# A dilated attention whose four engines run from a hand-written slot table: TensorE's scores and the turn of the maxima behind the weighted values, VectorE's split of the maxima ahead of the branch mix

## The reference

```python
q = (layernorm(x) @ Wq.T + bq).reshape(B, L, 16, 16)      # x: 8 x 256 x 256
k = (ctx @ Wk.T + bk); v = (ctx @ Wv.T + bv)               # the same shape
for sl, dr in ((256, 1), (512, 2), (1024, 4)):             # three branches
    # a head keeps every dr-th position; causal softmax over the kept ones
    o, lse = branch(q, k, v, sl, dr)
w = softmax(stack(lse), over the branches)
out = sum(o_b * w_b) @ Wo.T + bo
x = x + tanh(g_xattn[1]) * out
# the next part takes layernorm(x) and router logits of it
```

## Time and profile before

| | value |
|---|---|
| median of three runs | 878.72 us |
| lowest and highest | 876.07, 879.52 us |
| the profiled execution: its span, first to last instruction | 879.3 us |
| mean granted TensorE clock, as a share of full speed | 0.860 |
| PE matmul busy | 642.7 us, 73% of the span |
| DVE busy | 512.7 us, 58% |
| ACT busy | 415.4 us, 47% |
| POOL busy | 343.0 us, 39% |

### The profile page before, as it was taken

How to read it: one execution, slowest core, us unless ns; L and a number is a source line. 1 busy time by engine, 2 the same in 40 slices (tenths; PEclk the granted TensorE clock), 3 DMA queues, 4 the chain that set the end, 5 groups by cost and what they waited for, 6 DMA issues and landing times. The chain is left out here.

```text
span 879.3 us, 14726 instructions
## 1 busy us (share of the span) xinstructions
PE 642.7 (73%) x4856; PEld 476.7 (54%) x4856; DVE 512.7 (58%) x1634; ACT 415.4 (47%) x810; POOL 343.0 (39%) x474
## 2 busy tenths in 40 slices
PE   3988898288999999999124868877779630168794
PEld 2777786157767777877112445554445420046673
DVE  1477656655665566554015577777873438866562
ACT  1354431174685577556111556655656311056571
POOL 2233333376336434742212435434443130124553
PEclk9999999679999999999655789898888755579997
DMA  5253223256354435431211222231200122025542
GB/s 186 74 181 97 73 92 125 67 154 158 89 126 108 134 85 141 108 67 19 48 42 40 61 61 86 75 81 57 74 26 27 40 83 83 8 67 133 141 106 31
DMA packets 73871, 75.93 MB, mean 86 GB/s; under 512 B 8037, under 2 KB 66449, under 8 KB 73553
## 3 DMA queue, kind: packets, MB, share of 16 engines
q1 hardware_dynamic: 61217, 59.32, 21.4%
q0 software_dynamic: 10928, 15.57, 10.2%
q10 hardware_dynamic: 1664, 0.27, 0.2%
HBM read 52.20 MB, written 22.94 MB: 85 GB/s over the span
## 5 line engine op out<-in xcount | busy, mean ns | idle before, releaser
L1866 DVE CUSTOM_DVE_ANT_0 c_sn<-c_ps_s,k_mask 128x128 f32<-128x128 f32 (+1 forms) x256 | 75.8, 352 | 55.5 <-PE c_ps_s L2004 55.4
L1390 PE MATMUL b_ps_y<-b_w2h,b_hh 128*128 128x256 f16 x320 | 87.3, 273 | 6.4 <-DVE b_xl L1283 4.4
L1390 PE MATMUL b_ps_y<-b_w2h,b_hl 128*128 128x256 f16 x320 | 87.2, 273 | 0.0
L1390 PE MATMUL b_ps_y<-b_w2l,b_hh 128*128 128x256 f16 x320 | 87.2, 273 | 0.0
L1698 POOL TENSOR_SCALAR_AFFINE_SELECT c_pr<-c_pr 128x512 f32<-128x512 f32 x64 | 43.1, 674 | 112.9 <-ACT c_pr L1757 111.9
L1200 POOL DMA_INDIRECT res<-b_y,b_s_idx x40 | 69.3, 1732 | 41.8 <-ACT b_y L1242 33.4
L1274 DVE TENSOR_TENSOR b_hl<-b_h,b_hh 128x640 f16<-128x640 f32 x64 | 52.8, 825 | 38.6 <-ACT b_hh L1222 36.6
L1186 POOL DMA_INDIRECT e_xg<-rows,e_g_idx x35 | 38.2, 1093 | 87.9 <-DVE e_g_idx L1301 73.8
L2032 PE MATMUL c_ps_v<-c_pr,k_vx 128*64 128x256 f32 (+1 forms) x512 | 64.2, 378 | 5.4 <-POOL c_pr L1698 4.8
L1757 ACT ACTIVATE c_pr<-c_ps_t 128x768 f32<-128x768 f32 x64 | 51.7, 808 | 16.0 <-PE c_ps_t L2018 16.0
L1355 PE MATMUL b_ps_h<-b_xh,e_w1h 128*128 128x320 f16 x256 | 56.9, 304 | 2.7 <-ACT b_h L1217 1.6
(11 more groups left out here) (409 smaller groups left out, 1762.5 us busy)
## 6 DMA issues: line engine op xcount, KB each, us to landing
e_w<-in_L_ffn_W_dram SPq DMA_DIRECT2D x16, 1024.0 KB
d_w<-in_L_ffn_W_down_dram SPq DMA_DIRECT2D x8, 640.0 KB
k_ks<-kT SPq DMA_DIRECT2D x48, 64.0 KB, 2.7
c_qs<-q SPq DMA_DIRECT2D x48, 64.0 KB, 2.3
d_w<-in_L_ffn_W_up_dram SPq DMA_DIRECT2D x4, 682.0 KB, 5.8
rows<-a_rows SPq DMA_DIRECT2D x8, 264.0 KB, 2.6
rows<-c_rows SPq DMA_DIRECT2D x8, 264.0 KB, 2.2
a_x_in<-in_x_dram SPq DMA_DIRECT2D x8, 256.0 KB, 3.1
```

What stands on the lines that cost most here:

```text
L1390: last = pe.matmul(ps_y[(j + CT) % 2][:, 0:D], a, b[:, f, :], start=(f == 0 and k == 0), stop=(f == FC - 1 and k == 2))
L1866: dve.tensor_tensor_reduce(sn[r][:, a:b], ps_s[:, r, a:b], mask[:, a:b], -1.0, 3.0e38, ALU.add, ALU.min, mx[g % 2][:, q, r, j:j + 1]).then ...
```

## The change

Five edits, all in the written order:

1. PE: `scores` and the turn of the maxima stand behind `weighted` and `turned` of their slot, the turn ahead of the scores.
2. PE: the turn of `o` moves from the end of slot 4 to slot 5, right behind `by_keys` and ahead of `weighted`. ACT's `oT` moves to slot 5 too, ahead of `taken`.
3. DVE: the split moves from the start of slot 4 to slot 3, behind that slot's maxima; the maxima now come first in every slot. `mix` moves from slot 2 to slot 3 behind the split, `mix2` and `o` from slot 3 to slot 4, behind the maxima and the router's logits.
4. DVE: the statistics of e move from slot 4 to slot 0.
5. ACT: `mrow` stands behind `taken`. For this the turn of the maxima waits for this slot's `taken`, and `weighted` of slot 5 for `mrow`.

```diff
 # ScalarE
+                    if p == 5 and within(m):
+                        after(act, s_pot, m)
+                        after(act, s_po, m, 1)
+                        act.activation(oT[:], halves(ps_a), ACT.Copy).then_inc(s_oT, 1)
+                    if within(n):
+                        taken(n, p)
                     if p == 4 and within(g):
                         after(act, s_pm, g)
-                        if within(n):
-                            after(act, s_pv, n * HH + p)
                         landed(act, s_mst, g, 2)
                         act.activation(mrow[g % 2][:], ps_v[0:4 * HH, T:2 * T], ACT.Copy).then_inc(s_mrow, 1)
-                    if within(n):
-                        taken(n, p)
...
 # VectorE
-                    if p == 4 and within(g):
+                    if p < 4 and within(g):
+                        maxima(g, p + 4)
+                    if p >= 4 and within(f):
+                        maxima(f, p - 4)
+                    if p == 3 and within(g):
                         u = g % 2
...
-                    if p == 4 and within(e):
+                    if p == 0 and within(e):
                         landed(dve, s_ldx, e)
                         after(dve, s_nmr, e, 2)
                         stats(e, xs[e % 5], st[e % 2], s_st, mv[e % 2], s_mv, var[e % 2], s_var)
...
                             dve.tensor_tensor(aw[:], al[:], an[:], ALU.add).then_inc(s_aw, 1)
+                        if p == 3:
                             after(dve, s_aw, m)
...
-                        if p == 3:
+                        if p == 4:
                             after(dve, s_mix, m)
...
 # TensorE
+                if j == 5 and within(n + 1):
+                    after(pe, s_mrow, n + 1)
...
-                    if p < 4 and within(g):
-                        scores(g, p + 4)
-                    if p >= 4 and within(f):
-                        scores(f, p - 4)
-                    if p == 4 and within(g):
-                        after(pe, s_mlo, g)
-                        done(pe, s_av, n * HH + p)
...
+                    if p == 5 and within(m):
+                        after(pe, s_o, m)
+                        after(pe, s_xT, min(f, B - 1))
+                        after(pe, s_x3T, m, 1)
+                        turn(ps_a, o).then_inc(s_pot, 1)
                     if within(n):
                         weighted(n, p)
                     if p >= 1 and within(n):
                         turned(n, p - 1)
                     if p == 0 and within(m):
                         turned(m, HH - 1)
+                    if p == 4 and within(g):
+                        after(pe, s_mlo, g)
+                        done(pe, s_av, n * HH + p + 1)
...
+                    if p < 4 and within(g):
+                        scores(g, p + 4)
+                    if p >= 4 and within(f):
+                        scores(f, p - 4)
```

More of the change, by code:

```diff
@@ L1817, in step @@
                                            accum_out=lsum[:, j:j + 1]).then_inc(s_le, 1)
[L1818 to L1821, removed]
                     if p == 5 and within(e):
@@ L1887, in step @@
                             .then_inc(s_nmc, 1)
-                    if p < 4 and within(g):
-                        maxima(g, p + 4)
-                    if p >= 4 and within(f):
-                        maxima(f, p - 4)
                     if p == 0 and within(f):
@@ L2073, in step @@
                         turned(m, HH - 1)
+                    if p == 4 and within(g):
+                        after(pe, s_mlo, g)
+                        done(pe, s_av, n * HH + p + 1)
+                        for q in range(2):
+                            last = pe.matmul(ps_v[0:4 * HH, T + (1 - q) * P:T + (2 - q) * P],
+                                             mhl[g % 2][:, q, :, :, :].rearrange("p r l b -> p (r l b)"), ident_h[:],
+                                             start=True, stop=True)
+                        last.then_inc(s_pm, 1)
+                    if p < 4 and within(g):
+                        scores(g, p + 4)
+                    if p >= 4 and within(f):
+                        scores(f, p - 4)
                     if p == 2 and within(l):
@@ L2087, in step @@
                         last.then_inc(s_plg, 1)
-                    if p == 4 and within(m):
-                        after(pe, s_o, m)
-                        after(pe, s_xT, min(f, B - 1))
-                        after(pe, s_x3T, m, 1)
-                        turn(ps_a, o).then_inc(s_pot, 1)
                     if p == 5 and within(m):
```

## The result

| | before | after |
|---|---|---|
| median of the four runs of each in this comparison | 877.39 us | 893.43 us |
| lowest and highest | 876.0, 879.52 us | 891.24, 895.57 us |
| span of the profiled execution | 879.3 us | 891.9 us |
| mean granted TensorE clock | 0.860 | 0.856 |

The changed kernel is slower: the ratio of after to before is 1.0189, with a 95% interval from 1.015 to 1.0229. The forecast was 887.7 us (880.5 to 894). The direction and the main mechanism (PE's wait moves to `o`) came out as forecast. The loss was larger, 16 us between the medians for 9, and the median lies 0.6 us inside the upper end of the range.

A forecast was written before the change was run, and what follows sets the result against it. A loop between DVE's and PE's lists bounds the kernel; 9.3 (full steps) + 1 + 1.2 + 1 (other steps) - 3.5 (fill) = +9.0 us, giving 887.7 us, range 880.5 to 894.

The forecast's parts named there:

- The wait moves to `o`: PE idles about 4 us before slot 5's turn of `o`, released by DVE's `o`; no wait on the split.
- third rival: Slow clock lasts through slot 5's projection, DVE's half at 17.1 us: a full step +4.9 us, 894 us; chance 0.15.
- DVE's half: DVE's list from slot 0's maxima to `o`: 15.7 us, against 13.2 before.
- the stall goes and nothing takes its place: Rival: `o` is done when PE reaches slot 5; a step takes 22.6 us, the kernel 853 us; chance 0.05.
- the loop lengthens but little: Rival: DVE's half at its low end, 13.9 us; a step is +1.3 us, about 880 us; chance 0.14.
- The statistics at 1.35 us in DVE's half: e's statistics, moved into slot 0, add 1.35 us to DVE's half.
- The stall: PE takes some 11 us for four slots, reaches the turn of `o` about 4 us early and waits.
- PE's half: PE's list from the turn of `o` to DVE's next slot 0: 14.4 us, against 13.8 before.
- The full step: Batch-to-batch step: 15.7 + 14.4 us and a hand-over make 30.1 us, 3.1 more than 27.06; three steps +9.3.
- The step before them: Step without a router, before the three full steps: taken as +1 us, as it begins without a stall behind it.
- The fill: Before the first batch's values, e's statistics done in slot 0 while DVE idles: 3.5 us gained, of 0 to 4.8.
- three small terms: In PE's half: slow scores 0.4 us; slot 0's weighted and turned ahead of scores, 0.80 and 0.4; slot 7's scores 0.26.

The follow-up runs named there:

- The two experiments with the statistics: e's statistics back in slot 4 of the changed kernel: 904.73 us; e's statistics in slot 0 instead of slot 4 in the kernel before: 873.68 us.

## Why the prediction was right or wrong

**The wait moves to `o`: right.** The split and the turn of the maxima no longer hold PE, and the turn of `o` does, released by DVE's `o`. The third rival's condition (slow through the projection) came true in part: 3.03 us, between 1.89 and 3.78. The median of 893.43 us lies at its 894 rather than at the forecast's 887.7, though not by its sum: a full step lost 3.5 us and not 4.9, and DVE's half stayed at 15.54 us and not 17.1. That the stall goes and nothing takes its place is excluded by the 2.70 us ahead of the turn of `o`, and that the loop lengthens but little by full steps of 30.7 us.

**DVE's half, 15.7 us: right in its sum (15.54), by terms that cancel.** From slot 1's maxima to slot 2's, the first half of the weights and a group of maxima took 4.65 us, forecast 3.33: POOL's spread of the values now lies beside these products. The second half of the weights took 0.63, forecast 1.55, with POOL idle beside it, and `mix` 1.66, forecast 2.00; it had begun before POOL's next instruction. That the forecast of this half came within 0.2 us is therefore in part luck. One collision came the other way: ahead of slot 5's weighted values POOL's causal mask took 2.00 us, started 0.24 us behind `mix`; its neighbours take 0.64.

```profile
580.88 2.00 POOL L1698 TENSOR_SCALAR_AFFINE_SELECT c_pr<-c_pr 128x512 f32<-128x512 f32 x1 [3.35 <-ACT c_pr L1757]
585.26 0.64 POOL L1698 TENSOR_SCALAR_AFFINE_SELECT c_pr<-c_pr 128x512 f32<-128x512 f32 x1 [2.38 <-ACT c_pr L1757]
```

The mask ends at 582.88, half a microsecond behind `mix` (582.39). The Trainium skill, SBUF — State Buffer, "Who interferes with whom", has the two engines share a port pair as an exclusive lock; this trace agrees, with 2.00 us for 0.64.

**The statistics at 1.35 us in DVE's half: wrong.** They stand in a stretch in which DVE waits for PE's scores. The run with them back in slot 4 lost 11.3 us, and the step without e shows the same from the other side: there DVE's half was to shrink by 1.35 us, and it took 15.26 us (630.90 to 646.16), because DVE waited for slot 1's scores instead:

```profile
633.70 0.29 DVE L1864 CUSTOM_DVE_ANT_0 c_sn<-c_ps_s,k_mask 128x128 f32<-128x128 f32 x1 [0.99 <-PE c_ps_s L2003]
```

So the term for that step, +1.2, came out at +3.66 (its wait for `o` is 3.96 us, longer than in a full step). A list that is "almost solid" is not solid everywhere; what is put into its holes costs nothing, and taking it out gives nothing.

**The stall, about 4 us: 2.70.** PE came to the turn of `o` later than forecast. I gave it 11 us for its four slots; from slot 0's scores (569.18) to the end of by_keys (582.46) they take 13.3. They hold 3.29 us of waits, for 1.69 in the same slots of the kernel before: 0.58 us on ACT's probabilities (0.69 before), 0.37 and 0.78 on POOL's masks (0.20 and 0.28), 1.56 on DVE's maxima (0.52).

**PE's half, 14.4 us: 15.06.** To the turn of xn 8.45 us, forecast 8.1. The chain over `lrec`, the gates and the normalisation decides there, as forecast: from POOL's gates to the turn it took 3.40 us, forecast 3.41, and ACT's xn is done at 593.57, 0.05 us ahead of the turn (593.62). But PE itself came hardly sooner: its scores of slot 6 end at 593.49, because the projection took 3.03 us, and I had costed it at 1.89.

```profile
590.22 0.21 POOL L1728 TENSOR_TENSOR c_lp<-c_le,c_lrec 128x16 f32<-128x16 f32 x1 [4.32 <-DVE c_lrec L1904]
...
592.48 1.09 ACT L1749 ACTIVATE c_xn<-c_xs,c_nmr,c_rstd 128x256 f32<-128x256 f32 x2 [4.29 <-POOL c_nmr L1691]
...
593.15 0.34 PE L2003 MATMUL c_ps_s<-k_ks,c_qs 48*128 48x128 f16 x4
```

From the turn of xn on 6.61 us, forecast 6.33.

**The full step, +3.1: +3.5.** Three steps made +10.6, forecast +9.3. **The step before them, +1: +4.56.** I counted its missing router and no stall ahead of it. It had a stall of its own at the turn of `o`, 3.04 us, and began at the lower level: the product near its start took 3.78 us for 1.89. Its clock of 0.74 is the lowest of the six windows, and this is the worst term of the sum, 3.6 us too low.

**The fill, -3.5: -4.7** with the step behind it, counted from the stage's start and just within the bounds given. The two experiments with the statistics show that this is the fourth edit's gain. **The tail, +1: 0.0.** From the end of the step without e to the next part's first copy it is 74.56 us in both kernels. The steps missed by 3.6, 1.3 and 2.5 us; fill and tail give back 1.2 and 1.0 of these 7.4, and the stage came out at +14.15 for +9.0.

**Which edit.** The prediction never asked what each edit is worth by itself. Undoing edit 1 for the scores alone wins 24.6 us (19.6 in the stage, more than the 14.15 it had lost); the other four edits together with the turn of the maxima then make the kernel 0.6 to 1.2% faster than before. The loss is the scores' place. Undoing edit 2 alone wins 11.7 us, both 27.4, so the two overlap. Edits 3 and 5 were not tried alone. In the prediction the scores' place stood as three small terms (0.4, 0.80 with 0.4, and 0.26), 1.9 us in all in PE's half; they were the right places, but came to 3.14 us.

## What to carry to other kernels

When one engine's queue holds both work that another engine is starving for and work that only it needs, the first goes in front, even if it makes the second wait; a small matmul in front also shortens the wait for masks behind it (0.20 and 0.28 us here, for 0.37 and 0.78). Before pricing an operation that moves, ask whether its old and new places lie on a stretch in which the engine waits: the same 1.35 us cost 11 us over a run in one slot, fill included, and by estimate a quarter of a microsecond a step in another. And a change with several edits is best priced edit by edit, because one bad one can hide four good ones.

## What the runs showed of the hardware that was not expected

- The granted clock can stay at its lower level for most of a step, or not, with the same list: 30.7 us at 0.72 and 27.7 us at 0.88 in one run, behind stands that agree within 0.01 us. Nor does the length of a stand tell how long the level lasts: behind 2.70 us at the turn of `o` the projection took 3.03 us in the changed kernel; with slot 0's scores in front it took 3.29 us behind 2.69 and 1.99 behind 3.11.
- POOL's mask took 2.00 us instead of 0.64 when it began just behind DVE's big product; in the kernel before it began 0.19 us ahead of that product, took 0.65, and the product took 2.07 instead of 1.75.
